# Local attention layers: values a slot later, scores ahead of the turn of the probabilities, exponentials at the slot's end, norms of both halves in one step

## The chip, the core and the metric

The kernel runs on one core of a Trainium2 chip, in one launch. The metric is the device time of that launch in microseconds, as a median over runs. The engines are named as in the profile: PE is TensorE (PEld its weight load), DVE is VectorE, ACT is ScalarE, POOL is GpSimd, SP is SyncE.

## The reference, cut to what matters

The whole kernel is a decoder of twelve sublayers over x (4 sequences of 512 tokens, 128 features). The change is in the last sublayer alone, which holds six layers of local attention and a gated feed-forward part:

```
def attn_layer(x, Wqkv, qs, ksc, Wo):          # 16 heads of 64
    qkv = x @ Wqkv
    q, k, v = jnp.split(qkv, 3, -1)
    q = l2norm(q) * qs;  k = l2norm(k) * ksc
    q = q * cos * scale + rotate_half(q) * sin * scale
    k = k * cos * inv + rotate_half(k) * sin * inv
    out = local_attention(q, k, v)             # a query sees the 32 keys before it and itself
    return out.transpose(0, 2, 1, 3).reshape(b, n, INNER) @ Wo
...
for i in range(DEPTH):                         # DEPTH = 6
    x = attn_layer(shift_tokens(x), Wqkv[i], q_scale[i], k_scale[i], Wo[i]) + x
    x = ffn_layer(shift_tokens(x), ln_g[i], ln_b[i], W1[i], b1[i], W2[i], b2[i]) + x
```

ffn_layer is a layer norm, a matmul to 2 x 341 features, an exact gelu of one half times the other, and a matmul back to 128.

## The kernel before, in words

Each engine has a hand-written list of steps; engines meet only at counting semaphores (`wait_ge`, `then_inc`), and each engine runs its own list strictly in order. The work is cut into *slots*. A slot is one pair of heads (HP = 8 pairs) of one sequence of one layer; 8 slots make a batch, and 6 layers x 4 sequences make 24 batches, so 192 slots, numbered n = 8k + hp. In slot n every engine works on several pairs at once: projections and norms of pair n + 2, scores and exponentials of pair n + 1, probabilities and values of pair n. The feed-forward part of batch k - 1 (called f) is spread over the slots of batch k, a piece at a slot's end: slots 0 and 1 project the heads out (`project_out`), slot 2 turns the result to tokens (`turn_shifted`, `copy_tokens`, `token_stats`), slot 3 normalises them (`normal_tokens`, `turn_z`, `copy_z`), slot 4 makes the gate (`hidden`, `gelus` with two loads of activation tables), slot 5 the other factor and the product (`hidden`, `gated`), slot 6 goes back to 128 features (`feed_back`, `new_state`). Slot 7, and all slots of the first batch, have no such piece: plain slots.

The steps of a slot, by name and line of the profile:

- `qk` (L3015, PE) projects queries and keys, half j = 0 into bank 0 and j = 1 into bank 3. `square_part` (L3216, ACT) squares them, `rotate` (L3347 and L3350, DVE) multiplies by the cosine and sine tables, `norms` (L3359, DVE) sums the squares, `floor_norms` (L3366, DVE) bounds them, `inverse_norms` (L3222 and L3225, ACT) takes a logarithm and an exponential, `add_parts` (L2959, POOL) adds cosine and sine parts, `normalise` (L3379, DVE) multiplies by the inverse norm.
- `turn_qk` (L3031 and L3034, PE) transposes the normalised queries and keys into banks 6 and 7; `copy_qT` and `copy_kT` (L3235, L3239, ACT) copy them out.
- `direct` (L3060 and L3068, PE) makes scores in banks 0 and 2; `maxima` (L3387, DVE) finds the row maxima, `exps` (L3247, ACT, eight instructions, four for each half h) the exponentials and their sums, `inverse_sums` (L3372, DVE) and `divide_probs` (L2966, POOL) divide.
- `turn_probs` (L3047 and L3048, PE) transposes the probabilities into banks 4 and 5, `copy_probs` (L3257, ACT) copies them out, `project_v` (L3023, PE) and `copy_v` (L3231, ACT) make the values, `values` (L3089, PE) multiplies, again into banks 4 and 5, and `heads_out` (L3395, DVE) stores the result.

Three buffers tie the engines. Bank 0 holds both the projection's first half and the scores of h = 0, so a slot's projection waits for exponentials:

```
if j == 0:
    when(pe, "exp_done", (m - 2) * 2 * QT + QT)
```

Banks 4 and 5 hold both the turned probabilities and the values' result, so in `turn_probs(n)` stands `when(pe, "heads_done", n)`: the heads of pair n - 1 must have been stored. And `by_query` holds the exponentials until they are turned, so `exps` waits for `probs_turned`.

## Time and profile before

| what | value |
|---|---|
| median of 3 runs | 5088.73 us (5082.01 to 5094.36) |
| the profiled execution | 5093.95 us, its span 5092.2 us |
| busy share of the span | PE 75%, DVE 64%, ACT 55%, POOL 28% |
| first and last start of a local-layer exponential | 3064.3 us and 5038.8 us |
| granted TensorE clock, mean of the core | 0.830 of full speed |

Times in the rows are microseconds from the span's start. A row of the timeline gives start, duration, engine, line, instruction and shapes; x8 means eight like instructions in a row, merged, and the bracket at the end is how long the engine had been idle and which engine's work released it. Starts of two rows on one engine show its rate; a matmul's own duration reaches over the start of the next one.

### The profile page before, as it was taken

How to read it: one execution, taken by the hardware profiler on the slowest of the kernel's cores; microseconds unless marked ns; L12 is line 12 of the kernel's file. 1: busy time of each engine (PE TensorE's matmuls, PEld its weight loads, DVE VectorE, ACT ScalarE, POOL GpSimd, SP SyncE). 2: the span in 40 equal slices, each digit the busy share in tenths (PEclk: the TensorE clock that was granted, in tenths of full speed). 3: DMA queues.
4: the chain of work that ended last, by engine and by line, in shares of the span. 5: the costliest groups of instructions: out<-in, count | busy, mean ns of one | idle time of the engine just before them, and what ended most of it. 6: DMA issues, size and time to landing. Idle time of an engine off the chain costs nothing. (4 is left out here: it accounts for less than half of the span.)

```text
span 5092.2 us, 96128 instructions
## 1 busy us (share of the span) xinstructions
PE 3827.4 (75%) x32913; PEld 2248.5 (44%) x33140; DVE 3247.2 (64%) x6512; ACT 2786.9 (55%) x7830; POOL 1400.7 (28%) x2146
## 2 busy tenths in 40 slices
PE   2004768996767996786997668888888888888886
PEld 1003333333342222343443336666666666666664
DVE  8996444443427786435555327777787878777775
ACT  2034623442646875451224437777777777777775
POOL 0011101011112111210000135444555545454553
PEclk6556876555777988797997679999999999999998
DMA  1001133101213310302541000000000000000000
GB/s 45 0 0 33 35 81 69 32 14 27 41 34 82 83 27 14 68 10 78 142 136 34 5 23 28 5 9 24 5 28 5 6 27 5 9 24 5 28 5 11
DMA packets 139047, 170.17 MB, mean 33 GB/s; under 512 B 34607, under 2 KB 121755, under 8 KB 137412
## 3 DMA queue, kind: packets, MB, share of 16 engines
q1 hardware_dynamic: 138158, 164.06, 13.0%
q8 instruction: 261, 4.28, 0.4%
q14 instruction: 196, 1.61, 0.1%
q0 software_dynamic: 432, 0.23, 0.0%
HBM read 124.06 MB, written 32.89 MB: 31 GB/s over the span
## 5 line engine op out<-in xcount | busy, mean ns | idle before, releaser
L838 DVE TENSOR_REDUCE minus_max<-banks 128x1 f32<-128x512 f32 (+4 forms) x1152 | 622.5, 572 | 477.5 <-PE banks L667 467.0
L766 ACT ACTIVATE probs<-banks 128x512 f32<-128x512 f32 (+4 forms) x1152 | 615.8, 559 | 436.2 <-PE banks L635 426.8
L2966 POOL TENSOR_TENSOR loc_by_query<-loc_by_query,loc_inv_sums 128x512 f32<-128x512 f32 x386 | 470.1, 1236 | 560.2 <-DVE loc_inv_sums L3372 560.2
L2959 POOL TENSOR_TENSOR loc_cos_part<-loc_cos_part,loc_sin_part 128x512 f32<-128x512 f32 x388 | 488.2, 1277 | 414.5 <-DVE loc_sin_part L3350 413.8
L3247 ACT ACTIVATE loc_by_query<-banks,loc_minus_max 128x128 f32<-128x128 f32 x1544 | 540.6, 375 | 13.6 <-DVE loc_minus_max L3387 13.1
L3015 PE MATMUL banks<-loc_w_qkv,loc_shifted 128*128 128x256 f32 x1552 | 413.6, 414 | 169.4 <-ACT loc_by_query L3247 155.1
L635 PE MATMUL banks<-q_stack,k_stack 51*128 51x512 bf16 (+4 forms) x1152 | 444.4, 430 | 35.9 <-DMA q_stack<-max_rows 34.5
L667 PE MATMUL banks<-k_stack,q_stack 48*128 48x512 bf16 (+5 forms) x1536 | 443.3, 349 | 30.7 <-PEq L68 19.7
L3015 PEld LDWEIGHTS banks<-loc_w_qkv,loc_shifted 128*128 128x128 f32 x1552 | 310.0, 205 | 282.9 <-issue 229.4
L703 PE MATMUL banks<-probs,pair_rows 128*32 128x256 f32 (+1 forms) x4352 | 398.4, 448 | 8.6 <-issue 8.6
L3347 DVE TENSOR_TENSOR loc_cos_part<-banks,loc_table 128x512 f32<-128x512 f32 x388 | 265.5, 684 | 127.6 <-ACT loc_square L3216 126.5
L3247 ACT ACTIVATION_READ_ACCUMULATOR loc_by_query<-banks,loc_minus_max 128x1 f32 x1544 | 331.5, 215 | 0.0
L3216 ACT ACTIVATE loc_square<-banks 128x512 f32<-128x512 f32 x388 | 225.5, 604 | 108.2 <-PE banks L3015 107.4
L1349 ACT ACTIVATE gated<-banks 128x512 f32<-128x512 f32 x168 | 100.3, 597 | 336.7 <-PE banks L1310 336.7
L2012 PE MATMUL banks<-identity,srt_b 128*128 128x128 f32 x64 | 11.3, 320 | 344.6 <-DVE srt_b L2283 344.6
L3379 DVE TENSOR_TENSOR loc_rotated<-loc_cos_part,loc_inv_norm 128x512 f32<-128x512 f32 x388 | 267.5, 690 | 1.1 <-issue 0.6
L3350 DVE TENSOR_TENSOR loc_sin_part<-banks,loc_table 128x512 f32<-128x512 f32 x388 | 264.4, 681 | 0.0
L206 POOL TENSOR_SCALAR fin_shifted<-fin_moments 128x4 f32<-128x4 f32 x48 | 12.0, 250 | 892.1 <-DVE fin_moments L306 889.7
L800 POOL CAST max_parts<-minus_max 128x8 bf16<-128x8 f32 x192 | 36.7, 191 | 767.9 <-DVE minus_max L838 767.9
L3359 DVE TENSOR_REDUCE loc_norm_sq<-loc_square 128x8 f32<-128x512 f32 x388 | 246.4, 677 | 0.0
L1369 DVE TENSOR_TENSOR product<-gated,banks 128x512 f32<-128x512 f32 x168 | 115.4, 687 | 199.7 <-PE banks L1312 199.6
L635 PEld LDWEIGHTS banks<-q_stack,k_stack 51*128 51x128 bf16 (+1 forms) x1152 | 101.9, 97 | 294.1 <-issue 151.1
(491 smaller groups left out, 8783.6 us busy)
## 6 DMA issues: line engine op xcount, KB each, us to landing
expert_share<-limited_rows SPq DMA_DIRECT2D x136, 256.0 KB, 4.0
expert_w<-in_L_ffn_pairs_dram SPq DMA_DIRECT2D x84, 192.0 KB, 2.4
q_stack<-q_pieces SPq DMA_DIRECT2D x38, 384.0 KB, 6.3
loc_w_qkv<-in_L_ffn_Wqkv_dram SPq DMA_DIRECT2D x7, 1536.0 KB, 6.9
expert_share<-grouped_rows SPq DMA_DIRECT2D x32, 256.0 KB, 4.1
k_stack<-k_pieces SPq DMA_DIRECT2D x20, 384.0 KB, 9.6
q_pieces<-q_parts SPq DMA_DIRECT2D x19, 384.0 KB, 2.6
q_stack<-max_rows SPq DMA_DIRECT2D x384, 3.0 KB
```

What stands on the lines that cost most here:

```text
L635: nc.tensor.matmul(t_bank(n, k, e)[:, q0:S], k_stack[rows_e, k0:k0 + P], q_stack[rows_e, q0:S], start=plain, stop=True, skip_group_check=T ...
L667: ins = nc.tensor.matmul(d_bank(n, k, i)[:, at * nk:at * nk + keys], q_stack[rows_e, q * P:(q + 1) * P], k_stack[rows_e, 0:keys], start=pl ...
L703: ins = nc.tensor.matmul(o_bank[at:at + COLS, lo:hi], pair_rows[quad % 2][u][:, k, e, :], probs_of(2 * quad + u, k, e)[:, lo:hi], start=(k ...
L766: nc.scalar.activation(probs_of(n, k, e)[0:kn, q0:S], t_bank(n, k, e)[0:kn, q0:S], ACT.Exp, scale=scale).then_inc(s["exp_done"], 1)
L838: nc.vector.tensor_reduce(minus_max[:, n % 2, 1 - i, qs[0]:qs[0] + len(qs)], view, AX.X, ALU.max, negate=True).then_inc(s["max_done"], 1)
L2959: nc.gpsimd.tensor_tensor(cos_part[:, tiles, :], cos_part[:, tiles, :], sin_part[:, tiles, :], ALU.add).then_inc(s["summed"], 1)
L2966: nc.gpsimd.tensor_tensor(seen, seen, inv_sums[:, h, :].unsqueeze(1).unsqueeze(3).to_broadcast([P, 2, QT, BLOCK]), ALU.mult).then_inc(s["p ...
L3015: ins = nc.tensor.matmul(g.bank[3 * j][:, (t % 2) * QK:(t % 2 + 1) * QK], xs[:, t * P:(t + 1) * P], w_qkv[:, ds(at, QK)], start=True, stop ...
L3247: nc.scalar.activation(by_query[:, h, :, t % 2, r, :], score_banks[h][:, t * 2 * BLOCK:(t + 1) * 2 * BLOCK].rearrange("p (w k) -> p w k", ...
L3347: nc.vector.tensor_tensor(cos_part[:, tiles, :], g.bank[3 * j][:, :].rearrange("p (t d) -> p t d", t=2), table[:, 0, tiles, :], ALU.mult). ...
L3350: nc.vector.tensor_tensor(sin_part[:, tiles, :].rearrange("p t (e two d) -> p (t e) two d", two=2, d=half), src, table[:, 1, tiles, :].rea ...
L3379: nc.vector.tensor_tensor(groups(rotated[:, tiles, :]), groups(cos_part[:, tiles, :]), inv_norm[:, part].unsqueeze(2).to_broadcast([P, 8, ...
```

## The change

All four engines' lists of a slot are written in another order.

- PE: `project_v` comes right behind `qk`; then `turn_qk(n + 1)`, `values(n - 1)` (before: `values(n)`, at the slot's end), `direct(n + 1)`, and `turn_probs(n)` last. The waits for the gelu and the product in slots 5 and 6 are met in two parts, the first ahead of `project_v`.
- ACT: `copy_probs(n - 1)` begins the slot (before: `copy_probs(n)` in its middle), the second `square_part` stands behind the copies of turned queries and keys, and the exponentials of half 0 and half 1 stand around `inverse_norms`, which is one step for both halves of the projection.
- DVE: a slot begins with `inverse_sums` and `normalise` of what the slot before prepared; `heads_out(n - 1)` stands behind the rotations and the first `norms`, ahead of the first `maxima`; `floor_norms` is one step.
- POOL: the alternation of `divide_probs` and `prepare` is the same; `by_block` and `inverse_spread` (once a batch each) come one `divide_probs` earlier.
- At the end a last `values`, `copy_probs` and `heads_out` are added behind the loop.

```
@@ tensor
                         qk(n + 2, next_qk, 0)
                         qk(n + 2, next_qk, 1)
+                        if hp == LAST:
+                            pe.wait_ge(s["xv_done"], k + 2)
+                        if f is not None and hp == 5:
+                            pe.wait_ge(s["gelu_done"], f * NC + 1)
+                        if f is not None and hp == 6:
+                            pe.wait_ge(s["inner_done"], f * NC + 1)
+                        project_v(n + 1, next_v)
...
                         turn_qk(n + 1)
+                        if n > 0:
+                            values(n - 1, 1 - u)
+                        direct(n + 1)
                         turn_probs(n)
-                        if hp == LAST:
-                            pe.wait_ge(s["xv_done"], k + 2)
-                        project_v(n + 1, next_v)
-                        direct(n + 1)
-                        values(n, u)
@@ scalar
-                def inverse_norms(m, j):
-                    part = slice(8 * j, 8 * j + 8)
+                def inverse_norms(m):
...
+                        if n > 0:
+                            copy_probs(n - 1)
                         square_part(n + 2, 0)
-                        square_part(n + 2, 1)
                         copy_qT(n + 1)
                         copy_kT(n + 1)
-                        copy_probs(n)
+                        square_part(n + 2, 1)
                         copy_v(n + 1, 1 - u)
...
-                        inverse_norms(n + 2, 0)
-                        inverse_norms(n + 2, 1)
-                        exps(n + 1)
+                        exps(n + 1, 0)
+                        inverse_norms(n + 2)
+                        exps(n + 1, 1)
@@ vector
+                        inverse_sums(n, 0)
+                        normalise(n + 1, 0)
+                        normalise(n + 1, 1)
+                        inverse_sums(n, 1)
+                        rotate(n + 2, 0)
+                        rotate(n + 2, 1)
+                        norms(n + 2, 0)
...
                             heads_out(n - 1, before, parts)
-                        rotate(n + 2, 0)
-                        rotate(n + 2, 1)
-                        norms(n + 2, 0)
+                        maxima(n + 1, 0)
                         norms(n + 2, 1)
+                        floor_norms(n + 2)
+                        maxima(n + 1, 1)
...
-                        floor_norms(n + 2, 0)
-                        floor_norms(n + 2, 1)
-                        maxima(n + 1)
-                        normalise(n + 2, 0)
-                        inverse_sums(n + 1, 0)
-                        normalise(n + 2, 1)
-                        inverse_sums(n + 1, 1)
@@ gpsimd
+                        divide_probs(n)
                         prepare(n + 2)
-                        divide_probs(n + 1)
```

PE, from one `project_out` to the next, so slot 1 of a batch, before (loc_shifted is the projection's input, loc_by_block the values', loc_by_query the probabilities before their turn, loc_probs after it):

```order
L3015 MATMUL banks<-loc_w_qkv,loc_shifted 128x256 x4
L3031 MATMUL banks<-identity,loc_rotated 128x128 x4
L3034 MATMUL banks<-identity,loc_rotated 128x128 x4
L3047 MATMUL banks<-identity,loc_by_query 128x2x64
...
L3048 MATMUL banks<-identity,loc_by_query 128x2x64
L3023 MATMUL banks<-loc_w_qkv,loc_by_block 128x128 x4
L3060 MATMUL banks<-loc_band_direct,identity_bf 128x512 x2
L3068 MATMUL banks<-loc_kT,loc_qT 64x96 x16
L3089 MATMUL banks<-loc_probs,loc_v_1 64x96 x12
...
L3099 MATMUL banks<-loc_headsT,loc_w_o 128x512 x4
```

The same stretch of PE's list in the changed kernel (its line numbers are one lower there):

```order
L3014 MATMUL banks<-loc_w_qkv,loc_shifted 128x256 x4
L3022 MATMUL banks<-loc_w_qkv,loc_by_block 128x128 x4
L3030 MATMUL banks<-identity,loc_rotated 128x128 x4
L3033 MATMUL banks<-identity,loc_rotated 128x128 x4
L3088 MATMUL banks<-loc_probs,loc_v_1 64x96 x12
...
L3059 MATMUL banks<-loc_band_direct,identity_bf 128x512 x2
L3067 MATMUL banks<-loc_kT,loc_qT 64x96 x16
L3046 MATMUL banks<-identity,loc_by_query 128x2x64
...
L3047 MATMUL banks<-identity,loc_by_query 128x2x64
L3098 MATMUL banks<-loc_headsT,loc_w_o 128x512 x4
```

The turn of queries and keys has gone behind the value projection, and the turn of the probabilities from the slot's middle to its end.

ACT in the following slot (slot 2), between two pieces of the feed-forward part, before:

```order
L3264 ACTIVATE loc_mid_shifted<-loc_y_b 64x512
L3216 ACTIVATE loc_square<-banks 128x512 x2
L3235 ACTIVATE loc_qT<-banks 128x512
L3239 ACTIVATE loc_kT<-banks 128x512
L3257 ACTIVATE loc_probs<-banks 128x384 x2
L3231 ACTIVATE loc_v_1<-banks 128x512
L3222 ACTIVATE loc_norm_log<-loc_floored 128x8
L3225 ACTIVATE loc_inv_norm<-loc_norm_log 128x8
...
L3247 ACTIVATE loc_by_query,loc_sums<-banks,loc_minus_max 128x2x64 x8
L3268 ACTIVATE loc_mid_tokens<-banks 128x512
```

ACT in the same slot of the changed kernel:

```order
L3266 ACTIVATE loc_mid_shifted<-loc_y_b 64x512
L3259 ACTIVATE loc_probs<-banks 128x384 x2
L3221 ACTIVATE loc_square<-banks 128x512
L3238 ACTIVATE loc_qT<-banks 128x512
L3242 ACTIVATE loc_kT<-banks 128x512
L3221 ACTIVATE loc_square<-banks 128x512
L3234 ACTIVATE loc_v_1<-banks 128x512
L3249 ACTIVATE loc_by_query,loc_sums<-banks,loc_minus_max 128x2x64 x4
L3226 ACTIVATE loc_norm_log<-loc_floored 128x16
L3229 ACTIVATE loc_inv_norm<-loc_norm_log 128x16
L3249 ACTIVATE loc_by_query,loc_sums<-banks,loc_minus_max 128x2x64 x4
L3270 ACTIVATE loc_mid_tokens<-banks 128x512
```

The second square now stands behind the copies of the turned queries and keys.

DVE in slot 2 of the changed kernel, from the slot's first step to its last of attention (before, the slot began with L3395, then the rotations, and ended with L3379 and L3372 in turns):

```order
L3373 RECIPROCAL loc_inv_sums<-loc_sums 128x4
L3380 TENSOR_TENSOR loc_rotated<-loc_cos_part,loc_inv_norm 128x512 x2
L3373 RECIPROCAL loc_inv_sums<-loc_sums 128x4
L3350 TENSOR_TENSOR loc_cos_part<-banks,loc_table 128x512
L3353 TENSOR_TENSOR loc_sin_part<-banks,loc_table 128x512
L3350 TENSOR_TENSOR loc_cos_part<-banks,loc_table 128x512
L3353 TENSOR_TENSOR loc_sin_part<-banks,loc_table 128x512
L3362 TENSOR_REDUCE loc_norm_sq<-loc_square 128x8
L3395 COPY loc_headsT<-banks 128x512
L3387 TENSOR_REDUCE loc_minus_max<-banks 128x4
L3362 TENSOR_REDUCE loc_norm_sq<-loc_square 128x8
L3368 TENSOR_SCALAR loc_floored<-loc_norm_sq 128x16
```

The copy of the heads and the first maximum have moved behind both rotations and the first sum of squares.

## Rows read from the trace of the kernel before

**Rows 1.** The page, busy time of the engines over the span.

```profile
PE 3827.4 (75%) x32913; PEld 2248.5 (44%) x33140; DVE 3247.2 (64%) x6512; ACT 2786.9 (55%) x7830; POOL 1400.7 (28%) x2146
```

**Rows 2.** The tile loc_by_query: all exponentials; nanoseconds min/median/max, then first and last start.

```profile
L3247 ACT ACTIVATE loc_by_query<-banks,loc_minus_max x1544: 348/375/402, 3064.3 to 5038.8; 128x128 f32<-128x128 f32 x193
```

**Rows 3.** Timeline, ACT: first exponential of pairs 80, 81 and 88.

```profile
3879.64 0.35 ACT L3247 ACTIVATE loc_by_query<-banks,loc_minus_max 128x128 f32<-128x128 f32 x1
...
3887.97 0.35 ACT L3247 ACTIVATE loc_by_query<-banks,loc_minus_max 128x128 f32<-128x128 f32 x1
...
3961.46 0.35 ACT L3247 ACTIVATE loc_by_query<-banks,loc_minus_max 128x128 f32<-128x128 f32 x1
```

**Rows 4.** Timeline between the first two of these, DVE and then ACT.

```profile
3882.56 0.18 DVE L3372 RECIPROCAL loc_inv_sums<-loc_sums 128x4 f32<-128x4 f32 x1 [0.59 <-ACT loc_by_query L3247]
...
3885.63 1.27 DVE L3359 TENSOR_REDUCE loc_norm_sq<-loc_square 128x8 f32<-128x512 f32 x2
3886.82 0.49 DVE L3366 TENSOR_SCALAR loc_floored<-loc_norm_sq 128x8 f32<-128x8 f32 x2
...
3887.27 0.21 ACT L3222 ACTIVATE loc_norm_log<-loc_floored 128x8 f32<-128x8 f32 x1 [0.67 <-DVE loc_floored L3366]
```

**Rows 5.** Timeline, PE, slot 0 of a batch, from projection to projection.

```profile
3881.27 1.97 PE L3015 MATMUL banks<-loc_w_qkv,loc_shifted 128*128 128x256 f32 x8 [1.90 <-ACT loc_by_query L3247]
3883.07 0.60 PE L3031 MATMUL banks<-identity,loc_rotated 128*128 128x128 f32 x4
...
3884.01 0.30 PE L3047 MATMUL banks<-identity,loc_by_query 128*128 128x128 f32 x1
...
3884.91 1.06 PE L3023 MATMUL banks<-loc_w_qkv,loc_by_block 128*128 128x128 f32 x8
...
3887.84 3.70 PE L3099 MATMUL banks<-loc_headsT,loc_w_o 128*128 128x512 f32 x8
3891.38 0.81 PE L3015 MATMUL banks<-loc_w_qkv,loc_shifted 128*128 128x256 f32 x3
```

**Rows 6.** Timeline: pairs of rows in which one engine waits for the other.

```profile
3912.89 0.66 DVE L3395 COPY loc_headsT<-banks 128x512 f32<-128x512 f32 x1
...
3913.61 0.33 PE L3047 MATMUL banks<-identity,loc_by_query 128*128 128x128 f32 x1 [0.91 <-DVE loc_headsT L3395]
...
3928.33 1.02 DVE L3387 TENSOR_REDUCE loc_minus_max<-banks 128x4 f32<-128x384 f32 x2 [1.07 <-PE banks L3068]
...
3928.99 0.37 ACT L3247 ACTIVATE loc_by_query<-banks,loc_minus_max 128x128 f32<-128x128 f32 x1 [0.66 <-DVE loc_minus_max L3387]
...
3936.35 1.09 ACT L3216 ACTIVATE loc_square<-banks 128x512 f32<-128x512 f32 x2
...
3936.98 0.69 DVE L3347 TENSOR_TENSOR loc_cos_part<-banks,loc_table 128x512 f32<-128x512 f32 x1 [3.94 <-ACT loc_square L3216]
...
3947.29 0.66 PE L3031 MATMUL banks<-identity,loc_rotated 128*128 128x128 f32 x4 [1.52 <-DVE loc_inner L3441]
...
3948.48 0.59 ACT L3239 ACTIVATE loc_kT<-banks 128x512 f32<-128x512 f32 x1
```

**Rows 7.** Timeline: pieces of the feed-forward part in slots 2, 3 and 4.

```profile
3911.58 0.87 DVE L3424 BATCH_NORM_STATS2 loc_stats<-loc_mid_tokens 128x6 f32<-128x128 f32 x4 [0.31 <-ACT loc_mid_tokens L3268]
...
3917.04 1.25 DVE L3433 TENSOR_SCALAR loc_z<-loc_mid_tokens,loc_moments,loc_rstd 128x128 f32<-128x128 f32 x4
...
3928.89 2.81 PE L3122 MATMUL banks<-loc_zT,loc_pack 128*85 128x512 f32 x6
...
3931.91 1.28 ACT L3278 ACT_TABLE_LOAD   x1
```

**Rows 8.** Two windows (length, then busy PE, PEld, DVE, ACT, POOL; PEclk), and PE's timeline.

```profile
3917.00:3921.60 4.60, 2.07 (x38) 1.67 (x29) 3.76 (x12) 3.14 (x19) 1.16 (x2) 1.00 0.03 7
3921.70:3925.00 3.30, 3.30 (x13) 2.82 (x12) 2.60 (x6) 2.56 (x6) 1.98 (x3) 0.50 0.00 0
...
3920.73 2.86 PE L3015 MATMUL banks<-loc_w_qkv,loc_shifted 128*128 128x256 f32 x8 [1.73 <-ACT loc_by_query L3247]
```

More of the change, by code:

```diff
@@ L3199, in _ @@
                 f = BATCHES - 1
+                values(BATCHES * HP - 1, 1)
                 pe.wait_ge(s["v_copied"], BATCHES * HP + 1)
@@ L3331, in _ @@
                 f = BATCHES - 1
+                copy_probs(BATCHES * HP - 1)
                 lower_middle(f)
@@ L3381, in normalise, with maxima @@
                                             ALU.mult).then_inc(s["rotated_done"], 1)
[L3383 removed]
+                def maxima(m, h):
                     dve.wait_ge(s["direct_ready"], m + 1)
[L3385 to L3389 removed]
+                    when(dve, "exp_done", (m - 1) * 2 * QT + (h + 1) * QT)
+                    nc.vector.tensor_reduce(minus_max[:, :, h],
+                                            score_banks[h][:, :].rearrange("p (t j) -> p t j", t=QT)[:, :, WINDOW:2 * BLOCK],
+                                            AX.X, ALU.max, negate=True).then_inc(s["max_done"], 1)
                 def heads_out(n, hp, o_parts):
@@ L3509, in _ @@
                         norms(m, j)
-                    for j in range(2):
-                        floor_norms(m, j)
-                    if m == 1:
-                        maxima(0)
-                    for j in range(2):
-                        normalise(m, j)
-                    if m == 1:
-                        for h in range(2):
-                            inverse_sums(0, h)
+                    floor_norms(m)
+                    if m == 0:
+                        for j in range(2):
+                            normalise(m, j)
+                for h in range(2):
+                    maxima(0, h)
                 batch(0, None)
```

68 lines of the change are left out of this document (27 added, 41 removed).

## The prediction

> **What bounds the kernel now.** I read the page first: PE is the busiest engine, with 75% of the span [rows 1], so over the whole kernel no engine is full. The chain that ended last is no help here, since it followed only the final normalisation. So I asked where the local layers lie: their exponentials start between 3064.3 and 5038.8 [rows 2], 192 slots in 1975 us, 10.3 us a slot. The timeline gives a batch, from the first exponential of pair 80 to that of pair 88, 81.82 us, and a plain slot 8.33 us [rows 3].
>
> In a plain slot one closed loop sets the pace, between ACT and DVE. From the first exponential at 3879.64 the last sums are there at 3882.56 (2.92); then the reciprocal, the copy of the heads and four rotations take until 3885.63 (3.07, so 0.60 for each 512-wide step), two sums of squares until 3886.82 (1.19), the floors until the logarithm at 3887.27 (0.45), and two logarithms and two exponentials until 3887.97 (0.70) [rows 3, 4]. That is 8.33, all of it. PE isn't in this loop: it idles 1.90 before its projection [rows 5]. In slots 0, 1, 4 and 6 PE is the bound instead: with a head projection of 3.54 behind the attention work (3887.84 to 3891.38) a slot is 10.11 (3881.27 to 3891.38), and PE hardly waits [rows 5].
>
> **The change, part by part.** I set PE's start of `qk` to 0 and follow the new lists; a following start lies 0.16 before a matmul group's recorded end (3887.84 + 3.70 against 3891.38) [rows 5].
>
> 1. *PE's head of the slot.* `qk` takes 1.80, `project_v` 0.90 (1.06 less 0.16) [rows 5]. So `turn_qk` starts at 2.70; before it started at 1.80. `normalise` now comes at the slot's head on DVE, two steps behind a reciprocal, and is ready by about 1.6, earlier than that.
> 2. *From the turn to the second square.* The copy of the keys starts 1.19 behind the turn (3947.29 to 3948.48) [rows 6]. `square_part(., 1)` now stands behind it and starts 0.49 later, since ACT starts one 512-wide step each 0.49 (two squares 1.09, one 0.60), and DVE's second rotation starts 0.63 after that (3936.35 to 3936.98) [rows 6]. That is turn + 2.31. Before, this square needed only the projection.
> 3. *DVE behind it.* Two rotation steps 1.20, the first `norms` 0.60, so `heads_out` starts at turn + 4.11 and the first `maxima` at turn + 4.71. `values(n - 1)` and `direct(n + 1)`, which these two also need, are done before (the first right behind the turn, the second about 3.5 behind it). Making values a slot late and scores early therefore buys nothing: what reads them stands later in DVE's list.
> 4. *Back to PE, two ways.* The exponentials start 0.66 behind the maximum (3928.33 to 3928.99) and the next `qk` 1.63 behind their start (3879.64 to 3881.27) [rows 3, 5, 6]: turn + 7.00, a loop of **9.70 us**. Or over the banks: `turn_probs` starts 0.72 behind the start of `heads_out` (3912.89 to 3913.61) and takes 0.90 (3884.01 to 3884.91) [rows 5, 6]: PE is free at turn + 5.73, at **8.43**, and does the slot's extra piece after that. A slot is the longer of 9.70 and 8.43 + extra.
> 5. *Norms in one step.* This removes a floor, a logarithm and an exponential per slot, half of 0.70 on ACT and half of 0.49 on DVE [rows 3, 4]. In the new order ACT idles some 2.7 before its exponentials, and the floor lies beside them, so I cost it at nothing; were that cover gone it would be worth 0.35 x 192 = 67 us. The Trainium skill ("VectorE: DVE Perf Modes", section on the TRN2 errata) says that VectorE and ScalarE pay a fixed latency for each instruction and that one wide step pays it once: it speaks for this edit, and on the path it would give those 67 us back.
> 6. *POOL and DMA.* POOL's alternation is unchanged; all its work in the kernel is 1400.7 us [rows 1], under 7.3 a slot even if all of it were here, less than 9.70. Its two moved steps come once a batch beside waits of DVE. The number of edge transfers is the same, each now with a slot more before it is read, so nothing; if one were late it would hold `values`, which has over 2 us until `heads_out`.
>
> Slot by slot in a batch, at full clock. Slots 0 and 1: 8.43 + 3.54 = 11.97 each. Slots 2 and 7: 9.70 each (their extra is under 0.7). Slots 4 and 6: six matmuls of 512 columns, 2.81 less 0.16 [rows 7], 11.08 each. Slot 3: `token_stats` stands at the end of DVE's slot 2, now ahead of `normalise`. The four exponentials of half 0 take some 1.4 and the merged norms 0.35, so half 1 ends near 1.5 and the tokens are copied at 2.15; statistics 1.31 (3911.58 to 3912.89) [rows 6, 7], reciprocal and two normalisations 1.4: the turn starts at 4.90 instead of 2.70. The loop would end at 11.90, but `normal_tokens`, now behind both maxima, starts at 4.90 + 4.71 + 1.69 = 11.30, takes 1.30 [rows 7], and PE has `turn_z` (0.50) before the next projection: 13.10. Slot 5: ACT's two table loads and three gelus last 4.44 (3931.91 to 3936.35) [rows 6, 7] and, with the wait before them, reach to 4.71; then come `copy_probs` (0.74) and three steps of 0.49, so the second square is at 6.92, not 4.38; heads at 9.35, PE free at 10.97, plus 2.65: 13.62. Sum: 23.94 + 19.40 + 22.16 + 13.10 + 13.62 = 92.22, against 81.82.
>
> Sum over the kernel: 23 batches x 10.40 = 239; the first batch's eight plain slots 8 x (9.70 - 8.33) = 11; the end, where `copy_probs` and `values` of the last pair now come behind everything, 5. Together **255 us** at full clock.
>
> 7. *The clock.* The granted clock was 1.00 from 3917.00 to 3921.60 while PE was busy 2.07 of 4.60, and 0.50 (1.2 GHz) for the 3.3 us from 3921.70, in which the projection took 2.86 instead of 1.97 [rows 5, 8]. At 1.2 GHz 3.3 us of back-to-back work cost 1.65. The new order puts more such gaps into PE's list: in a plain slot PE is idle about 1.6 ahead of `turn_probs` and 1.3 behind it, with 0.9 of work between; in slot 3 it waits 2.1 for the turn, 1.6 for the heads and 2.0 for z. My 92.22 holds no fall at all (81.82 holds one). From none to five falls a batch are open; I take two to three, because slots 3 and 7 have gaps like the row's and slots 2 and 5 perhaps: 2.5 x 1.6 x 23 = **92 us**, as PE's head of the slot is on both ways of step 4.
>
> The sum is 255 + 92 = 347 on the profiled execution's own 5093.95, that is 5441; its time is 5.2 above the median of the three runs, so against the median I forecast **5435 us**, 7% slower.
>
> **The rivals.**
>
> *The clock stays high* (0.15). A gap of 1.90 before the projection was followed by one of the usual length, 1.97 [rows 5]. If the new ones are too, only step 4 counts: 5089 + 255 = 5344. The Trainium skill ("TensorE: Matmul & The Clock Gate", section "Why this matters for your kernels") warns of long idle gaps between matmul bursts alone; by it short gaps like these cost nothing but themselves and this rival is right. The fall at 3921.7, after two short ones, speaks against it.
>
> *A fall in nearly every slot* (0.15): five or more a batch, 5 x 1.6 x 23 = 184, so 5528.
>
> *A looser chain* (0.12): a step of 2 to 4 is shorter or overlaps, say 0.7 a slot, 134 us less: about 5300.
>
> *Faster* (0.06): the chain from the turn to the end of `turn_probs` doesn't bind, and PE runs its list without a gap. Its work is then 6.5 in a slot, and a plain slot about 7.9 (scores, maximum 0.66, exponentials 1.63); the two plain ones of a batch and the first eight save 0.43 each (23 us), slots 2, 3 and 5 some 2 a batch (46): about 5020. It decides if that chain takes under 4.4 instead of 5.73 (10.40 / 8 = 1.30 less), that is, if the second square didn't wait for the turn. Against it stands the order of ACT's list, which no row makes looser. *No change to speak of* 0.02.
>
> **How the numbers follow.** The forecast case, 5380 to 5500, has 0.50. With the high-clock case, the nearer half of the many-falls case and of the looser chain the range is 5310 to 5535. A difference of 0.2% (10 us) is about what a measurement tells from none: faster 0.06, same 0.02, slower 0.92.
>
> **What would show it.** In the new profile: a plain slot near 9.7 between first exponentials, or 11 with a slow clock; DVE waiting for ACT's square ahead of the second rotation; PE waiting for the stored heads ahead of `turn_probs` in nearly all slots; ACT waiting for the maxima. PE's busy time in microseconds rises only by what the low clock adds. I am wrong if the second rotation starts under 4 us behind the projection's start, or if PE doesn't wait for the heads.

## The result and the profile after

The changed kernel took 5496.87 us (median of four runs, 5490.79 to 5514.31), the kernel before 5091.55 us on the same chip (5082.01 to 5112.48): a ratio of 1.078 [1.074, 1.082]. The forecast of 5435 us had the right side and, but for one step, the right mechanism, and was 62 us short.

Two lines of the page of the changed kernel: busy time by engine, and the group of the step that gives the turn its input.

```profile
PE 3963.0 (72%) x32913; PEld 2315.5 (42%) x33140; DVE 3316.6 (60%) x6314; ACT 2704.4 (49%) x7442; POOL 1383.6 (25%) x2144
...
L3380 DVE TENSOR_TENSOR loc_rotated<-loc_cos_part,loc_inv_norm 128x512 f32<-128x512 f32 x386 | 377.7, 1019 | 13.0 <-ACT loc_inv_norm L3229 13.0
```

PE has exactly the instructions of [rows 1] and 136 us more busy time. 107 of them lie in the local part, where PE spent 147 us more at 1.2 GHz than before; work at half speed takes twice its time, so at most half of the 147 is added busy time. What the rest of the 107 is was not looked into. Every engine's share of the span fell: the time went into waits. The list of waits of the changed kernel names them (who waited for whom: us, times, longest).

```profile
ACT loc_by_query L3249 <- PE banks L3047: 517.6, 191, 2.9
...
DVE loc_cos_part L3350 <- ACT loc_square L3221: 439.1, 271, 5.0
...
PE banks L3046 <- DVE loc_headsT L3395: 274.5, 189, 1.5
...
PE banks L3030 <- DVE loc_rotated L3380: 107.8, 116, 3.9
```

The second and the third are the two that the prediction named: DVE's rotation waits for ACT's square, and PE waits for the stored heads before `turn_probs`, in 189 of 192 slots. The first and the last it had not named: it expected ACT to wait for the maxima, and ACT waits for the turned probabilities.

The timeline of slot 1 of a batch, of four engines, in order of time, answers to [rows 5, 6]; slot 0 ran the same steps.

```profile
4372.45 1.89 PE L3014 MATMUL banks<-loc_w_qkv,loc_shifted 128*128 128x256 f32 x8
4373.34 2.11 DVE L3380 TENSOR_TENSOR loc_rotated<-loc_cos_part,loc_inv_norm 128x512 f32<-128x512 f32 x2
4373.51 1.40 POOL L2966 TENSOR_TENSOR loc_by_query<-loc_by_query,loc_inv_sums 128x512 f32<-128x512 f32 x1 [5.22 <-DVE loc_inv_sums L3373]
...
4375.60 0.63 PE L3030 MATMUL banks<-identity,loc_rotated 128*128 128x128 f32 x4 [0.37 <-DVE loc_rotated L3380]
...
4376.76 0.59 ACT L3242 ACTIVATE loc_kT<-banks 128x512 f32<-128x512 f32 x1
4377.23 0.60 ACT L3221 ACTIVATE loc_square<-banks 128x512 f32<-128x512 f32 x1
...
4377.87 0.69 DVE L3350 TENSOR_TENSOR loc_cos_part<-banks,loc_table 128x512 f32<-128x512 f32 x1 [1.16 <-ACT loc_square L3221]
...
4379.67 0.68 DVE L3395 COPY loc_headsT<-banks 128x512 f32<-128x512 f32 x1
4380.26 0.55 DVE L3387 TENSOR_REDUCE loc_minus_max<-banks 128x4 f32<-128x384 f32 x1
4380.40 0.33 PE L3046 MATMUL banks<-identity,loc_by_query 128*128 128x128 f32 x1 [1.50 <-DVE loc_headsT L3395]
...
4381.10 0.37 ACT L3249 ACTIVATE loc_by_query<-banks,loc_minus_max 128x128 f32<-128x128 f32 x1 [2.77 <-PE banks L3047]
4381.33 3.60 PE L3098 MATMUL banks<-loc_headsT,loc_w_o 128*128 128x512 f32 x8
```

Read it from the turn (4375.60). The keys are copied at 4376.76, the square that now stands behind them starts at 4377.23, the rotation at 4377.87, two steps and a sum of squares later the heads at 4379.67 (turn + 4.07; predicted 4.11), the turn of the probabilities at 4380.40 (turn + 4.80; 4.83), and PE is free at 4381.33 (turn + 5.73; 5.73). That chain came as predicted, within 0.04. What is late is the turn itself: 3.15 behind the projection's start, not 2.70.

Two windows of the changed kernel (length; busy PE, PEld, DVE, ACT, POOL; granted clock), and the same stretch of the kernel before (from the second batch to the last exponentials); then PE's row at the head of a slot 0.

```profile
3177.30:5347.40 2170.10, 1643.68 (x18703) 1248.18 (x18878) 1494.50 (x2915) 1304.21 (x4599) 902.07 (x770) 0.95 0.04 12
4359.30:4362.60 3.30, 3.30 (x10) 2.64 (x9) 2.84 (x5) 2.49 (x11) 1.86 (x2) 0.50 0.00 0
```

```profile
3135.60:5036.40 1900.80, 1622.92 (x19551) 1252.81 (x19736) 1497.97 (x3233) 1442.00 (x5177) 953.38 (x805) 0.98 0.04 14
```

```profile
4358.94 3.47 PE L3014 MATMUL banks<-loc_w_qkv,loc_shifted 128*128 128x256 f32 x8 [1.25 <-ACT loc_by_query L3249]
```

The mean clock fell from 0.98 to 0.95. Counted stretch by stretch, the local part behind its first batch ran some 215 us at 1.2 GHz, before some 92. Such a stretch lasts 3.4 us or twice that; counted in units of 3.4 us, as everywhere below, that is 2.7 falls a batch against 1.2. The row lies in one of them: PE waited 1.50 before `turn_probs`, 1.25 before the projection, and the projection then took 3.47 instead of 1.89.

### The profile page after: what moved, and what is told of

It reads as the page before. It is cut to its first block and busy times, and to the rows that moved or that the text cites. A ratio compares the mean times of both kernels' runs of the same rounds, so it can differ in the third digit from the quotient of the medians.

```text
span 5512.5 us, 95580 instructions
## 1 busy us (share of the span) xinstructions
PE 3963.0 (72%) x32913; PEld 2315.5 (42%) x33140; DVE 3316.6 (60%) x6314; ACT 2704.4 (49%) x7442; POOL 1383.6 (25%) x2144
## 5 line engine op out<-in xcount | busy, mean ns | idle before, releaser
L2966 POOL TENSOR_TENSOR loc_by_query<-loc_by_query,loc_inv_sums 128x512 f32<-128x512 f32 x384 | 442.6, 1155 | 788.1 <-DVE loc_inv_sums L3373 788.1
L3014 PE MATMUL banks<-loc_w_qkv,loc_shifted 128*128 128x256 f32 x1552 | 444.5, 438 | 75.4 <-ACT loc_by_query L3249 60.9
L3014 PEld LDWEIGHTS banks<-loc_w_qkv,loc_shifted 128*128 128x128 f32 x1552 | 333.6, 220 | 188.8 <-issue 127.1
L3046 PE MATMUL banks<-identity,loc_by_query 128*128 128x128 f32 x768 | 190.2, 288 | 274.7 <-DVE loc_headsT L3395 274.5
L3380 DVE TENSOR_TENSOR loc_rotated<-loc_cos_part,loc_inv_norm 128x512 f32<-128x512 f32 x386 | 377.7, 1019 | 13.0 <-ACT loc_inv_norm L3229 13.0
L3249 ACT ACTIVATION_READ_ACCUMULATOR loc_by_query<-banks,loc_minus_max 128x1 f32 x1544 | 312.9, 203 | 0.0
L3238 ACT ACTIVATE loc_qT<-banks 128x512 f32<-128x512 f32 x193 | 115.8, 600 | 369.0 <-PE banks L3030 369.0
L3362 DVE TENSOR_REDUCE loc_norm_sq<-loc_square 128x8 f32<-128x512 f32 x388 | 262.4, 677 | 0.0
L3022 PEld LDWEIGHTS banks<-loc_w_qkv,loc_by_block 128*128 128x128 f32 x1544 | 226.4, 212 | 39.1 <-ACT loc_gate L3284 23.1
L3046 PEld LDWEIGHTS banks<-identity,loc_by_query 128*128 128x128 f32 x768 | 108.0, 141 | 311.0 <-DVE loc_headsT L3395 310.9
```

Source lines behind the costliest of these rows:

```text
L2966: nc.gpsimd.tensor_tensor(seen, seen, inv_sums[:, h, :].unsqueeze(1).unsqueeze(3).to_broadcast([P, 2, QT, BLOCK]), ALU.mult).then_inc(s["p ...
L3014: ins = nc.tensor.matmul(g.bank[3 * j][:, (t % 2) * QK:(t % 2 + 1) * QK], xs[:, t * P:(t + 1) * P], w_qkv[:, ds(at, QK)], start=True, stop ...
L3046: nc.tensor.transpose(before[:, :, 0:BLOCK], by_query[:, h, 0, t].rearrange("p r k -> p (r k)"), ident)
L3249: nc.scalar.activation(by_query[:, h, :, t % 2, r, :], score_banks[h][:, t * 2 * BLOCK:(t + 1) * 2 * BLOCK].rearrange("p (w k) -> p w k", ...
L3380: nc.vector.tensor_tensor(groups(rotated[:, tiles, :]), groups(cos_part[:, tiles, :]), inv_norm[:, part].unsqueeze(2).to_broadcast([P, 8, ...
```

## The experiments

In each timed run one profile gives the batch (first exponential of one batch to that of the next, mean of 22): 82.57 us in the kernel before, 98.64 in the changed one. "Without a fall" below means the median of those slots, from projection to projection, in which the clock stayed at 1.00.

**1. The second square back ahead of the copies of queries and keys** (in the changed kernel).

```diff
 square_part(n + 2, 0)
+square_part(n + 2, 1)
 copy_qT(n + 1)
 copy_kT(n + 1)
-square_part(n + 2, 1)
```

> The changed kernel with one move on ScalarE: the second square stands ahead of the copies of the turned queries and keys again. Theory A (the chain turn, copy of keys, second square, second rotation, stored heads, turn of probabilities sets every slot): in the changed kernel the heads are stored 4.07 us behind the turn and the turn starts 3.15 behind the projection, so 7.2; with the square free the second rotation follows the first, both end near 5.5, the heads start near 6.1, 1.1 us earlier in seven slots of a batch and 0.3 in slot 5: 24 x 8.0 = 190 less, about 5300 us (5270 to 5330). Rival B (PE's list is slow by itself, through the low clock and the late turn, the square's place does not matter): 5480 to 5510.

5240.52 us, ratio 1.026 [1.022, 1.030], batch 88.47. One line of ACT's list is worth 0.052 of the time before, 264 us, where I expected 190. The timeline of slot 1:

```profile
4202.39 1.89 PE L3014 MATMUL banks<-loc_w_qkv,loc_shifted 128*128 128x256 f32 x8
...
4206.58 0.68 DVE L3350 TENSOR_TENSOR loc_cos_part<-banks,loc_table 128x512 f32<-128x512 f32 x1
...
4208.37 0.67 DVE L3395 COPY loc_headsT<-banks 128x512 f32<-128x512 f32 x1
4209.10 0.33 PE L3046 MATMUL banks<-identity,loc_by_query 128*128 128x128 f32 x1 [0.25 <-DVE loc_headsT L3395]
```

DVE's rotation no longer waits, the heads come at 5.98 instead of 7.22 behind the projection, and PE's wait ahead of `turn_probs` shrinks from 1.50 to 0.25. With that wait went half of the falls of the clock: 1.4 a batch instead of 2.7, with 0.97 as the mean clock of the local part. Slot by slot without a fall a batch is 8.4 us shorter, where I expected 8.0; the rest of the 10.2 goes with the clock.

**2. The copy of the heads between the two rotations** (in the changed kernel).

```diff
 rotate(n + 2, 0)
-rotate(n + 2, 1)
-norms(n + 2, 0)
 if n > 0:
...
     heads_out(n - 1, before, parts)
+rotate(n + 2, 1)
+norms(n + 2, 0)
 maxima(n + 1, 0)
```

> The changed kernel with one move on VectorE: the copy of the heads stands between the two rotations instead of behind them and the first norms. Theory A: only the way over the banks is shortened. PE is free 7.1 us behind the projection instead of 8.9, so slots 0, 1, 4 and 6 with their long pieces become 1.7 to 1.8 shorter and slot 5 by 1.1; the loop over the exponentials keeps its 9.8 to 10, because the maxima come only 0.3 earlier: 9 a batch, 23 x 9 = 210 less, about 5290 us. Plain slots stay near 9.7. Rival C (the loop over the exponentials decides in all slots): 0.3 a slot, 58 less, 5440.

5346.76 us, ratio 1.047 [1.043, 1.051], batch 91.81: between the two expectations. In slot 1 the heads are there at 5.12 and `turn_probs` starts at 6.38 instead of 7.95, when PE's own work in front of it is done. But the first maximum still stands behind the late square, so the exponentials move only from 8.65 to 8.16. Of the two ways back to PE that the prediction priced, the one over the banks is cut, and the one over the exponentials goes on: two lines of this kernel's list of waits, and PE at the head of a slot 0.

```profile
ACT loc_by_query L3249 <- DVE loc_minus_max L3387: 427.8, 191, 4.0
...
PE banks L3014 <- ACT loc_by_query L3249: 114.8, 53, 3.6
```

```profile
4247.91 3.65 PE L3014 MATMUL banks<-loc_w_qkv,loc_shifted 128*128 128x256 f32 x8 [2.33 <-ACT loc_by_query L3249]
```

ACT waits for the maxima now, as the prediction had it for the changed kernel. PE's wait for the exponentials is 2.33 there instead of 1.25, 114.8 us in all instead of 60.9, and its clock fell 3.6 times a batch, with 0.93 as the mean over the local part. That took back part of what the shorter way gave.

**3. Both.** The edit of experiment 1, and the copy of the heads right behind both rotations, ahead of the first sum of squares:

```diff
 rotate(n + 2, 1)
-norms(n + 2, 0)
 if n > 0:
...
     heads_out(n - 1, before, parts)
+norms(n + 2, 0)
 maxima(n + 1, 0)
```

> Both moves: second square ahead of the copies, heads stored right behind the two rotations and ahead of the first norms. Theory A: the two ways shrink together, heads at 5.5 behind the projection, PE free at 7.15, loop over the exponentials 9.0; a batch near 84 at full clock and 87 with falls of the clock, against 98.6 now: about 5230 us. If this is as slow as the better of the two alone, one of the two ways was not shortened. It should still be slower than the kernel before (5090), because projection, value projection and turn stand in series ahead of the scores.

5197.65 us, ratio 1.018 [1.014, 1.021], batch 85.36, falls 1.0 a batch. That is faster than the 5230 I expected. The two orders explain 13.3 of the 16.1 us that a batch had lost.

**4. The reciprocals of the sums behind both normalisations** (in the changed kernel). They release POOL's division of the probabilities.

```diff
-inverse_sums(n, 0)
 normalise(n + 1, 0)
 normalise(n + 1, 1)
+inverse_sums(n, 0)
 inverse_sums(n, 1)
```

> The changed kernel with one move on VectorE: both normalisations stand ahead of the first reciprocal of sums, so that GpSimd's division of the probabilities starts behind them. Theory D (the second normalisation waits until GpSimd's division, which reads SBUF, is done; that is why two of them take 2.11 us where they take 1.26 beside small GpSimd steps): the pair returns to 1.3, the turn starts at 2.7 instead of 3.15 to 3.7 behind the projection in slots 1, 2, 6 and 7, 2.2 a batch, 50 less: about 5445 us. Rival E (the pair is slow by its place behind a reciprocal or by its data): pair still 2.1, 5480 to 5510.

5437.76 us, ratio 1.063 [1.057, 1.068], batch 95.23: 3.4 less, though the falls rose from 2.7 to 3.2 a batch. The tile `loc_rotated` (nanoseconds min/median/max) in the changed kernel and then in this one:

```profile
L3380 DVE TENSOR_TENSOR loc_rotated<-loc_cos_part,loc_inv_norm x386: 654/681/1534, 3075.3 to 5441.7; 128x512 f32<-128x512 f32 x193
```

```profile
L3380 DVE TENSOR_TENSOR loc_rotated<-loc_cos_part,loc_inv_norm x386: 657/684/722, 3088.6 to 5366.7; 128x512 f32<-128x512 f32 x193
```

And this kernel's timeline of slot 1:

```profile
4335.30 1.89 PE L3014 MATMUL banks<-loc_w_qkv,loc_shifted 128*128 128x256 f32 x8
4336.11 1.28 DVE L3380 TENSOR_TENSOR loc_rotated<-loc_cos_part,loc_inv_norm 128x512 f32<-128x512 f32 x2
4337.56 2.04 POOL L2966 TENSOR_TENSOR loc_by_query<-loc_by_query,loc_inv_sums 128x512 f32<-128x512 f32 x2 [6.43 <-DVE loc_inv_sums L3373]
4337.92 0.60 PE L3030 MATMUL banks<-identity,loc_rotated 128*128 128x128 f32 x4
```

In the changed kernel the pair of normalisations took 2.11 (4373.34) while POOL's division ran from 4373.51 to 4374.91; here the pair takes 1.28, before POOL starts, the longest of all 386 is 0.72 instead of 1.53, and the turn starts at 2.62, as soon as PE is ready. This edit alone would leave rival E, since the pair also left its place behind the reciprocal. The trace of the changed kernel settles it: 163 of its 386 normalisations took over 0.8, and a division of POOL was running beside every one of them. In slot 3 the reciprocal stands in the same place, but POOL was still at the token statistics and began its division only at 4401.28; the pair took its short time, here as in all but one of the 24 batches:

```profile
4399.15 1.26 DVE L3380 TENSOR_TENSOR loc_rotated<-loc_cos_part,loc_inv_norm 128x512 f32<-128x512 f32 x2
```

The late turn was thus two instructions in each other's way, DVE's normalisation (two operands in SBUF) and POOL's division. The Trainium skill ("SBUF — State Buffer", section "Who interferes with whom") states that a VectorE instruction with two SBUF inputs contends with a GpSimd instruction that reads SBUF, that this contention is an exclusive lock, and that the order of issue decides which of the two waits. The trace agrees: the second normalisation ends only 0.54 behind POOL's first division, and that division, started beside the first normalisation, took 1.40 instead of 1.04.

**5. Norms in one step alone, in the order of before** (the functions `inverse_norms(m)` and `floor_norms(m)` of the change in the kernel before).

```diff
-inverse_norms(n + 2, 0)
-inverse_norms(n + 2, 1)
+inverse_norms(n + 2)
 exps(n + 1)
...
-floor_norms(n + 2, 0)
-floor_norms(n + 2, 1)
+floor_norms(n + 2)
```

> The kernel before with one part of the change alone: floors, logarithms and exponentials of the norms in one step for both halves, order kept. The steps lie on the loop of the plain slots there (2.92 + 3.07 + 1.19 + 0.45 + 0.70 = 8.33): one floor less is 0.2 and a pair less on ScalarE 0.35, so a plain slot should fall to about 7.8. Theory F (it pays only where this loop sets the slot: the eight slots of the first batch and slots 2, 7 and perhaps 3 of the others; elsewhere TensorE's list does): 8 + 23 x 2.5 slots x 0.5 = 33 less, 0.6 to 0.7% faster. Rival: it pays in all 192 slots, 100 less, 2% faster; or nowhere, because something else follows at once.

5078.19 us against 5104.71, ratio 0.994 [0.992, 0.996], batch 81.30. The size is what theory F gave, but not from where it had it. A plain slot of the kind of [rows 3, 4], 8.33 long before, should have fallen to about 7.8 and took 8.31. At the end of such a slot, DVE and then ACT:

```profile
4033.16 1.02 DVE L3380 TENSOR_REDUCE loc_minus_max<-banks 128x4 f32<-128x384 f32 x2
...
4033.82 0.37 ACT L3245 ACTIVATE loc_by_query<-banks,loc_minus_max 128x128 f32<-128x128 f32 x1 [0.20 <-DVE loc_minus_max L3380]
```

The logarithm (at 4033.16) and the exponential of the norms (at 4033.41) are one each now, 0.21 and 0.22 long where each of the four took 0.19 to 0.21, but ACT then waits for the maxima, which stand behind the floors on DVE and start when they did before (7.66 behind the first exponential, 7.64 before). The loop of [rows 3, 4] has this second way through the maxima, only 0.02 shorter, and [rows 4] didn't show it. The first batch took 68.1 us instead of 71.4, but not by a gain in each slot: five of its eight slots changed by 0.03 at most, and the two that hold 3.0 of the 3.2 are those in which the kernel before had a fall that this run had shorter or not at all. Experiment 11, with the same lists in this batch, took 71.3. The gain of 1.27 a batch lies, without a fall, in slots 2, 3 and 7 (0.15, 0.16 and 0.23); about half of it goes with the clock, which fell 0.7 times a batch instead of 1.2. That the one-step norms cause the fewer falls is not shown.

**6. Scores ahead of the turn of the probabilities alone, values in their own slot** (in the kernel before).

```diff
 turn_qk(n + 1)
-turn_probs(n)
...
 project_v(n + 1, next_v)
 direct(n + 1)
+turn_probs(n)
 values(n, u)
```

> The kernel before with another part alone: the turn of the probabilities behind the scores, on TensorE's list only; values stay in their own slot. The value multiplication must then wait for the copies of probabilities turned just ahead of it, and ScalarE's copy of the values waits behind these. By the rows of before: scores end 4.9 behind the projection, the turn 5.75, its copies 6.2, values 7.2 instead of 6.6, and the norms' logarithm 6.7 instead of 6.0: about 0.6 to 0.7 in nearly every slot, 100 to 130 slower (5210 to 5240 against 5112 on this chip). If it is equal or faster, the early scores are worth something that my account leaves out.

5284.14 us, ratio 1.033 [1.030, 1.036], batch 89.11: worse than I expected. The timeline of a slot 1, PE and ACT:

```profile
4263.33 0.89 PE L3068 MATMUL banks<-loc_kT,loc_qT 64*64 64x96 f32 x32
...
4264.91 0.87 ACT L3257 ACTIVATE loc_probs<-banks 128x384 f32<-128x384 f32 x2 [2.24 <-PE banks L3048]
4265.93 0.84 PE L3089 MATMUL banks<-loc_probs,loc_v 64*64 64x96 f32 x32 [0.68 <-ACT loc_probs L3257]
```

PE turns the probabilities at 4.99 behind the projection (2.60 before), ACT waits 2.24 for them, PE then 0.68 for ACT's copies, and ACT's exponentials, behind those copies, start at 7.68 instead of 6.5. The early scores are of no use, since ACT isn't there to take them. It also suggests what the values a slot later are for in this order: they would take away PE's 0.68. No run has that step alone.

**7. Experiments 3 and 4 together** (edits as above).

> The changed kernel with three moves: second square ahead of the copies, heads stored right behind the rotations, both normalisations ahead of the reciprocals. Against the two moves (batch of 85.4) the turn comes at 2.62 instead of 3.15, 3.7, 3.2 in slots 1, 2 and 7, and slots 3 and 5 hardly change: 1.5 to 2 a batch, 40 less, 1.0175 falls to about 1.009 of the kernel before. Rival: the reciprocals now come so late that the division of the probabilities holds their turn; then no gain.

5123.56 us, ratio 1.003 [1.001, 1.005], batch 82.66, falls 0.5 a batch. Three moves, of one activation, one copy and one reciprocal, give back 15.98 of the 16.07 us a batch. Values a slot late, scores early, exponentials last and the norms in one step are all still in it. So what the change cost were those three orders. But this kernel still stands 0.9% behind that of experiment 5, which has only the one-step norms: the late values and the early scores together buy nothing here.

**8. The turn ahead of the value projection** (in the kernel of experiment 7).

```diff
-project_v(n + 1, next_v)
...
 turn_qk(n + 1)
+project_v(n + 1, next_v)
 if n > 0:
     values(n - 1, 1 - u)
```

> As the three moves, and on TensorE the turn of queries and keys stands ahead of the value projection again. The normalised queries are there at about 2.1 behind the projection's start, so the turn starts at 2.15 instead of 2.62, its copies and the scores come 0.5 earlier: about 0.4 in most slots, 60 to 80 less than the three moves, ratio 0.995 to 1.0. If the value projection then delays something (copy of the values behind it), the gain is smaller.

5216.76 us, ratio 1.021 [1.019, 1.024], where I had expected a gain. This kernel's timeline of slot 1:

```profile
4207.70 1.89 PE L3014 MATMUL banks<-loc_w_qkv,loc_shifted 128*128 128x256 f32 x8
4209.94 0.63 PE L3030 MATMUL banks<-identity,loc_rotated 128*128 128x128 f32 x4 [0.35 <-DVE loc_rotated L3380]
...
4211.83 0.84 PE L3088 MATMUL banks<-loc_probs,loc_v 64*64 64x96 f32 x32
...
4212.81 0.69 DVE L3395 COPY loc_headsT<-banks 128x512 f32<-128x512 f32 x1 [0.49 <-PE banks L3088]
```

The turn starts at 2.24, 0.38 earlier than in experiment 7, behind a wait of 0.35 that the value projection had covered. The values start at 4.13 instead of 3.59, and DVE, now early enough, waits for them: heads at 5.11 instead of 4.56. In this slot what sets the heads had passed from the turn to the values, and I had still costed the turn. Falls rose as well, from 0.5 to 1.3 a batch.

**9. Token statistics behind the normalisation, and the tokens' normalisation ahead of the second sums** (slot 3, in the kernel of experiment 7; POOL's step for them is moved likewise).

```diff
 normalise(n + 1, 1)
+if f is not None and hp == 3:
+    token_stats(f)
...
 maxima(n + 1, 0)
+if f is not None and hp == 3:
+    normal_tokens(f)
 norms(n + 2, 1)
...
-if f is not None and hp == 3:
-    normal_tokens(f)
...
-if hp == 2:
-    token_stats(f)
```

> The three moves (1.0031 of the kernel before) and, in slot 3 alone, the statistics of the tokens behind the two normalisations, the normalised tokens between the two maxima, and GpSimd's inverse spread behind its division. In the three moves slot 3 is 12.53 us long, because the turn starts 4.84 behind the projection (statistics stand ahead of the normalisations) and z is the last thing before TensorE goes on. By the same chain the turn should return to 2.7, the heads come near 6, z near 8.9 and the slot end at 9.5 to 10: 2.5 to 3 a batch, 55 to 70 less, ratio 0.990 to 0.992. If the slot stays over 12, something else than the order of these steps held it.

5111.78 us, ratio 1.002 [1.000, 1.005], not told apart from experiment 7. Slot 3 did shrink, from 12.53 to 10.72, but slot 4 grew from 9.34 to 10.91. The timeline at their border, POOL, DVE and PE:

```profile
4173.66 2.49 POOL L2959 TENSOR_TENSOR loc_cos_part<-loc_cos_part,loc_sin_part 128x512 f32<-128x512 f32 x2
...
4174.23 2.51 DVE L3433 TENSOR_SCALAR loc_z<-loc_mid_tokens,loc_moments,loc_rstd 128x128 f32<-128x128 f32 x4
...
4176.80 0.66 PE L3113 MATMUL banks<-identity,loc_z 128*128 128x128 f32 x4 [2.40 <-DVE loc_z L3433]
4177.30 2.86 PE L3014 MATMUL banks<-loc_w_qkv,loc_shifted 128*128 128x256 f32 x8
```

PE waits 2.40 for the normalised tokens. They came late because their four instructions on DVE took 2.51 beside POOL's additions, where they took 1.11 in experiment 7 with POOL idle: the interference of experiment 4 a second time, with another instruction of DVE. The median over the 24 batches is 2.58. That is most of why slot 3 ended at 10.72 and not at 9.5 to 10.

Slot 4 didn't grow by the clock, though the projection in this row runs at 1.2 GHz: it took 10.91 in the twelve batches without a fall and 11.00 in the eleven with one. It grew because the second sums, the second maxima and with them the exponentials of half 1 now stand behind the tokens. These exponentials start 0.81 behind the projection of slot 4 (in experiment 7 1.39 ahead of it), and the first square of that slot at 3.60 instead of 1.79. What the one slot gave the next took.

**10. ACT's second table load moved under a wait** (in the kernel of experiment 9). After the gelus ACT loads the tables of logarithm and exponential; the load stood at the end of `gelus` and now stands in slot 5 ahead of the exponentials.

```diff
-        nc.scalar.preload_act_table_set("natural_log_exp_and_others")
...
 lower_half((k + 1) % B)
+if f is not None:
+    nc.scalar.preload_act_table_set("natural_log_exp_and_others")
 exps(n + 1, 0)
```

> As before that, and in slot 5 the load of the second activation table stands ahead of the first exponentials instead of ahead of the copies and squares, which need no table of their own; ScalarE waits for the maxima there anyway. Slot 5 is 13.02, with the second square at 6.2 behind the projection; 1.28 earlier it should give 1.0 to 1.3 a batch, 23 to 30 less, ratio 0.985 to 0.987. Rival: the turn, which waits for the last gelu at 3.7, or the product in slot 5 holds the slot, and nothing changes.

5078.59 us, ratio 0.997 [0.995, 0.999]. Slot 5 went from 13.34 to 11.89. The step of 0.5% is what I had expected; the whole is 1% short, by the miss of experiment 9.

**11. One-step norms and the moved table load, in the order of before** (experiment 5 with the edit of 10, the load ahead of `inverse_norms(n + 2)` in slot 5).

> The kernel before in its own order, with the two edits that paid: norms in one step for both halves (0.9939 alone) and in slot 5 the second activation table loaded ahead of the logarithm instead of ahead of the squares. There ScalarE waited 1.34 for the floors, so the load of 1.28 should be covered and the squares, rotations and floors come up to 1.28 earlier: 0.9 to 1.2 a batch, 20 to 28 less, ratio 0.988 to 0.990. Rival: slot 5 is held by the turn, which waits for the last gelu, or by the load in its new place: 0.993 to 0.994 as without it.

5030.34 us against 5108.55, ratio 0.985 [0.982, 0.988], batch 79.30: the fastest of all, and faster than both kernels. ACT's timeline in slot 5 of experiment 5 and of this kernel, and one window of each over the slot 4 before it:

```profile
4160.51 1.28 ACT L3283 ACT_TABLE_LOAD   x1
4161.81 1.09 ACT L3216 ACTIVATE loc_square<-banks 128x512 f32<-128x512 f32 x2
...
4166.94 0.21 ACT L3221 ACTIVATE loc_norm_log<-loc_floored 128x16 f32<-128x16 f32 x1 [1.35 <-DVE loc_floored L3360]
```

```profile
4150.54 1.83 ACT L3280 ACTIVATE loc_gate<-banks,loc_pack 85x512 f32<-85x512 f32 x3
4152.26 1.07 ACT L3216 ACTIVATE loc_square<-banks 128x512 f32<-128x512 f32 x2
...
4156.45 1.28 ACT L3297 ACT_TABLE_LOAD   x1
4157.74 0.22 ACT L3221 ACTIVATE loc_norm_log<-loc_floored 128x16 f32<-128x16 f32 x1
```

```profile
4146.20:4157.00 10.80, 10.80 (x109) 8.10 (x109) 7.88 (x16) 8.43 (x33) 5.75 (x5) 0.84 0.02 5
```

```profile
4139.40:4148.60 9.20, 9.14 (x107) 6.77 (x109) 7.62 (x15) 7.85 (x31) 5.43 (x5) 1.00 0.03 6
```

The squares follow the gelus at once, with no load between them, and the load fills the 1.35 that ACT had waited for the floors. Slot 5 shrinks from 12.32 to 11.14. Slot 4 also shrinks, from 10.11 to 9.48 in the mean, though nothing in it was touched. Without a fall it takes 9.36 in both kernels; experiment 5 had a fall there in twelve of 23 batches (10.8 long, the window with 0.84), this kernel in two. In all, 0.1 falls a batch are left of 0.7. Why PE's clock holds there now isn't settled, so of the 2.0 us a batch only the 1.18 of slot 5 can be put down to the covered load.

## Why the prediction was right, and where its size was off

**Steps 2 to 4, the chain and its two ways back: right.** Heads at turn + 4.07 (4.11), `turn_probs` at + 4.80 (4.83), PE free at + 5.73 (5.73). Experiments 1 to 3 show the cause: with the square and the heads back in place 13.3 of 16.1 us a batch return. In the loop over the exponentials these are released by the turned probabilities, not by the maxima (191 times in the list of waits), which adds 0.13: turn + 5.50 instead of + 5.37. So the way over the exponentials also runs through the stored heads. (The sentence under the last list of "The change" is wrong about the first maximum: before, it stood behind both sums and the floors, and now it stands ahead of the second sum.) That late values and early scores buy nothing agrees with experiments 6 and 7. A plain slot at full clock took 9.82 (predicted 9.70), and 11.50 with one fall of the clock (predicted "or 11"), as the starts of ACT's first exponentials in the first batch of the changed kernel have it, of which two, 9.82 apart, are these:

```profile
3133.32 0.37 ACT L3249 ACTIVATE loc_by_query<-banks,loc_minus_max 128x128 f32<-128x128 f32 x1 [2.77 <-PE banks L3047]
...
3143.14 0.37 ACT L3249 ACTIVATE loc_by_query<-banks,loc_minus_max 128x128 f32<-128x128 f32 x1 [2.77 <-PE banks L3047]
```

**Step 1, the head of the slot: this failed.** "Ready by about 1.6, earlier than that" took the normalisations at the length that they had before (0.69 in the mean). But the reciprocals now release POOL's division just ahead of the normalisations, which came to 1.02 in the mean. In slots 1, 2, 6 and 7 the turn started at 3.15, 3.73, 3.28 and 3.21, not at 2.70: 2.6 us a batch, 59 over 23. Experiment 4 shows it: with the reciprocals behind, 3.4 us a batch return, and its slots without a fall add up to 91.8, against the 92.22 of the prediction. Step 6 had cleared POOL by its share of time alone; that it gets in DVE's way was in no step.

**Step 5, the norms: no harm, but the price on the path was wrong.** Costed at nothing under the cover of the exponentials' wait, which no run contradicts; 67 us if on the path. The one plain slot whose loop [rows 3, 4] give lost 0.02 instead of 0.35, because the maxima stand right behind the floors (experiment 5). "That is 8.33, all of it" was true of the one way and left out the other. The 27 us that the edit gave in the order of before (0.6%) came from other slots and from the clock.

**Step 7, the clock: right in kind and place, its size nearly so.** 2.5 falls a batch at 1.6 were predicted, 4.0 us. 2.7 came, in most batches behind the gaps of slots 3 and 7 (at the head of slot 4 in 20 of 23, of slot 0 in 16), as the prediction had it, and hardly any behind slots 2 and 5. They cost less than their number times 1.68, because a second unit often lay over a wait: the slots without a fall add up to 95.0 us, 3.6 less than the mean batch. (Of slots 3 and 4 only one and three are without a fall.) Experiment 1, where the gap of 1.50 is 0.25, has no fall left at the head of slot 0; but more than this gap differs there, so what brings a fall is not shown. In the first batch, where the sum had none, six of eight slots were longer than 9.82 by one fall or more: 91.4 us instead of 71.4, 20 more where 11 were predicted.

**The sum.** The batches gave 23 x 16.07 = 370, the first batch 20, the end 8: 398 where 347 were predicted. Of the excess of 51, the batch without falls gives 64 (95.0 against 92.22 each, 2.6 of it the turn), the first batch 9 and the end 3. Two terms went the other way, which was luck and hid part of the miss: the clock by 8 (3.6 against 4.0), and 17 because the average batch of before was 0.75 longer than the one that I read. The profiled execution of the changed kernel also entered its local part 21.6 later than that of before, in layers that the change doesn't touch; the medians differ by 405.

**The rivals.** The clock stayed high: not so, though the gaps at the end of slot 7 were of 1.50 and 1.25 only. A fall in nearly every slot: nearly true of the first batch alone. A looser chain, and faster: the chain took what its rows gave, turn + 5.73, far from the 4.4 at which it would not have bound.

## What to carry to other kernels

Where an instruction is moved in an engine's list, ask which other engine's result stands just ahead of its new place: the square cost 264 us because it had gone behind two copies that wait for a matmul, though its own input was long there. A loop of waits that adds up to a slot's length need not be the only one: before pricing a shorter step, ask what else ends just behind it (experiment 5). Each wait that is removed must be priced against the one that comes last next (experiments 8 and 9), and work with no input of its own, like a table load, belongs into a wait that is there already. An engine with a low share of busy time can still block another: look at the duration of single instructions where two engines' lists newly overlap, not only at the sum (experiments 4 and 9).

## What the runs showed that was not expected

- A normalisation of two 128x512 operands takes 0.68, and up to 1.53 when POOL's division starts ahead of it; moving one reciprocal, a step of 0.17, behind it was worth 3.4 us a batch. The four instructions that normalise the tokens took 1.11 with POOL idle and 2.51 beside its additions.
- The falls of the clock changed with edits far from them: a wait of 1.50 cut to 0.25 went with half as many (experiment 1), a shorter chain that left PE idle elsewhere with 3.6 a batch instead of 2.7 (experiment 2), an earlier turn with 3.2 (experiment 4), and a table load moved in slot 5 with a slot 4 nearly free of them (experiment 11). In the changed kernel's slot 0, 3.3 us at 1.2 GHz followed waits of only 1.50 and 1.25.
- Squares and copies ran right behind gelus with no table load between them. One load took 1.28, and ACT's next instruction started 1.29 to 1.30 behind its start.
